# Flamingo gated block on one Trainium2 core: the first normalisation split in natural layout and transposed by a DMA, in a straight program

## The chip, the cores and the metric

The kernel runs on one core of one Trainium2 chip. A core has five engines that work side by side and signal each other with semaphores: PE (TensorE, matmuls and transposes, results to PSUM), DVE (VectorE), ACT (ScalarE), POOL (GpSimd) and SP (SyncE, which here only starts DMAs). The metric is device time in microseconds (us) of one execution, lower is better.

## The reference, cut to what matters

Four sequences of 512 rows of width 512 (2048 rows). Each row's token chooses one of four experts, and the weights of expert e are `ctx_w[e]` (512 x 512), used for all three of its products. Then a small mixture with eight experts of rank 16 follows.

```python
def _layernorm(x, axis=-1, eps=1e-05):
    m = jnp.mean(x, axis=axis, keepdims=True)
    v = jnp.var(x, axis=axis, keepdims=True)
    return (x - m) / jnp.sqrt(v + eps)
# first part, hidden_states = layernorm(x); Wg = Wu = Wd = ctx
for e in range(E):                                   # E = 4
    g = jax.nn.silu(jnp.einsum('bsd,fd->bsf', hidden_states, Wg[e]))
    u = jnp.einsum('bsd,fd->bsf', hidden_states, Wu[e])
    y = jnp.einsum('bsf,df->bsd', g * u, Wd[e])
    out = jnp.where((expert_ids == e)[..., None], y, out)
x = x + jnp.tanh(g_xattn[0]) * out
# second part, on layernorm(x): top 2 of 8 gates w, then
h = jax.nn.relu(jnp.einsum('betd,edr->betr', x, Wd) + bd)     # rank 16
eo = jnp.einsum('betr,erd->betd', h, Wu) + bu
x = x + jnp.tanh(g_ffn[0]) * jnp.einsum('bte,betd->btd', w, eo)
```

## The kernel before, in words

The rows are sorted by expert into 16 tiles of 128 rows (T = 16). A tile that holds rows of two experts is worked on once for each, so there are 19 pairs of tile and expert (NP = T + E - 1). POOL gathers the rows of a tile into `xs` by an indirect DMA and scatters them back at the end.

All products are made of fp16 parts. A factor is split into a high part (rounded to fp16) and a low part (what the rounding left), and a product is three matmuls for each of four blocks of 128: high x high, high x low, low x high (`split_product`, L603 to L605).

For pair k the work is as follows.

- **a(k)**: POOL computes mean and rstd of the tile (`rstd`, L456 to L458) from DVE's `statistics1`. ACT writes the normalised rows `h` (L824). PE transposes them into `ps_hT` (L677), four transposes. ACT copies the high part `hT_hi` from there (L810) and DVE subtracts for the low part `hT_lo` (L1074). PE multiplies (a(k), into `ps_a`).
- ACT takes silu of `ps_a` (L805), DVE multiplies (`prod`, L1068), PE transposes `prod` (L624), ACT and DVE split it (`pT_hi` L783, `pT_lo` L1104).
- **y(k)**: PE multiplies by the expert again (into `ps_y`) and DVE adds the result to the rows (`add_y`, L1086).
- The second part of a tile follows LATE = 3 pairs later: DVE `statistics2` (L1095, L1099), POOL rstd, ACT `h2` (L796, called h in the profile), PE transposes it (`ps_h2T`, L685), split on ACT and DVE (L815, L1110), PE `hidden_product` (L632 to L634), the gates on DVE, ACT (tanh, L801) and POOL (`choice`), PE transposes the weighted hidden values (L697, L698), PE `low_rank_out` (L642 to L645) and DVE adds (L1117).

The order on each engine is written out by hand: `step(i)` has its own list on each engine, and pairs and tiles stand in it with offsets. In step i PE makes, in this order, the hidden product of tile i-6, the transposes of `prod` i-1, a(i), the low-rank output of tile i-7, the transposes of h(i+1), those of h2(i-5), y(i-1) and the small transposes L697 and L698. ACT writes h(i+2) at the end of its step i. DVE makes `hT_lo`(i+1) between `product`(i) and the low part of h2. Each engine runs its list in order, and an instruction that waits holds up all that stand behind it.

The steps up to 6 or so are written one by one, with the preparation of the weights between them: PE transposes the expert weights (L551), ACT takes squares for a scale (L740) and the high parts `w_hi` (L752), DVE the low parts `w_lo` (L952). The later steps go through `pipeline`, which makes hardware loops of two steps for each round; in them the number of the pair is in a register, and column addresses and semaphore values are computed from it. In such loops, DVE writes a cell `gate_cell` (L1049) to carry a second wait ahead of an instruction, and the arrival of tile t of x is passed on by SP through the counter `x_in`.

SP's queue holds, in order: the tokens, the expert weights 0 to 2, a wait for gather 0, the expert weights 3, a wait for gather 1, the two gates, waits for gathers 2 and 3, the eight loads of the small weights of the second part (L397 to L404, semaphore `s_small`), and then the waits for the other gathers. DVE waits for all eight small loads in `router_bias` (L1002), ahead of its step 1, whose first instruction is `pT_lo`(0).

Of the kernel before, what the change touches and what calls it, by code (L numbers as in the profile page):

```python
# [6 lines left out]
def bass_flamingo_gated_kernel(  # L7
# [53 lines left out]
    with ctx:  # L61
# [127 lines left out]
        hT_hi = sb("hT_hi", [P, KC, P], fp16)  # L189
        hT_lo = sb("hT_lo", [P, KC, P], fp16)  # L190
# [122 lines left out]
        def pipeline(eng, step, first, pairs, tiles):  # L313

            def work(i):

                return ([(some(NP, off, i), i + off == 0) for off in pairs]
                        + [(some(T, off, i), i + off == 0) for off in tiles])

            end = max(NP - min(pairs), T - min(tiles))  # L320
            while first < end:
                last = first + 1
                while last < end and work(last) == work(first):
                    last += 1
                if last == first + 1:
                    step(first, first)
                else:
                    odd = (last - first) % 2
                    if odd:
                        step(first, first)  # L330
# [48 lines left out]
        def _(sp):  # L379
# [161 lines left out]
        def _(pe):  # L541
# [70 lines left out]
            def second_product(k, e):  # L612
# [119 lines left out]
        def _(act):  # L732
# [43 lines left out]
            def step(i, i0, meanwhile=None):  # L776
# [29 lines left out]
                if some(NP, 1, i0):  # L806
                    k = i + 1
                    act.wait_ge(hT_done, k + 1)
                    wait_last(act, a_done, k)
                    a(hT_hi[:, :, :], ps_hT[:, :, :], ACT.Copy).then_inc(hT_hi_done, 1)  # L810
# [453 lines left out]
```

## Time and profile before

| | us |
|---|---|
| Median of three runs | 203.82 (203.39 to 203.85) |
| Span of the profiled execution, first to last instruction | 201.4 |
| PE busy in it | 175.0 (87%) |
| DVE busy | 155.7 (77%) |
| ACT busy | 111.9 (56%) |
| POOL busy | 99.7 (50%) |

The time of the profiled execution outside the profiler's span is not recorded by itself; the median of the runs stands 2.4 us above the span, and that is what lies around it.

A group of instructions in the profile has the line, the engine, the operation and the tiles that it writes and reads, then count, busy time, mean duration, and what ended the idle time ahead of it. Matmuls overlap each other, so a PE row of 0.38 us takes less room in the queue: the starts of two neighbours tell how much. PEclk or the granted clock is 1.00 where TensorE runs at its upper level, 2.4 GHz.

### The profile page before, as it was taken

To read this page: it belongs to the slowest core of one execution; us is meant where nothing else is said; L and a number is where in the kernel's file an instruction comes from. 1 tells how busy PE (TensorE), PEld (TensorE's weight loads), DVE (VectorE), ACT (ScalarE), POOL (GpSimd) and SP (SyncE) were. 2 spreads that over 40 slices of the span, in tenths; PEclk is the share of its full clock that TensorE was granted. 3 is DMA by queue.
4 is the path that set the end of the run, shared out by engine and by line. 5 is a ranking of instruction groups with operands and counts; after the bars stand their busy time and mean duration, and the time that the engine had idled before them with its cause. 6 is when DMAs were issued, how large, how long until landed. Compare 5 with 4: busy or idle time off the path is not lost.

```text
span 201.4 us, 4382 instructions
## 1 busy us (share of the span) xinstructions
PE 175.0 (87%) x1074; PEld 104.0 (52%) x1075; DVE 155.7 (77%) x523; ACT 111.9 (56%) x224; POOL 99.7 (50%) x246
## 2 busy tenths in 40 slices
PE   1576896999997989999999999999999999976560
PEld 1564463655553656656656556655665655534310
DVE  4859696697768799889888998797877878678640
ACT  2596599884287166473665726547265561545200
POOL 4478846427246366375553735516244162445641
PEclk9999999999999999999999999999999999999955
DMA  5947572101210201203101011011010100101121
GB/s 135 370 163 231 205 216 69 52 5 20 86 55 0 52 0 52 59 0 104 55 0 54 0 52 52 2 52 52 0 54 0 52 20 33 52 0 55 52 104 52
DMA packets 6784, 13.43 MB, mean 67 GB/s; under 512 B 2392, under 2 KB 2520, under 8 KB 6768
## 3 DMA queue, kind: packets, MB, share of 16 engines
q0 software_dynamic: 2560, 8.39, 12.6%
q1 hardware_dynamic: 4208, 4.86, 7.3%
q8 instruction: 6, 0.10, 0.2%
q14 instruction: 10, 0.08, 0.2%
HBM read 9.06 MB, written 4.19 MB: 66 GB/s over the span
## 4 chain that ended last, share of the span: by engine, by line
PE 44%; issue 18%; POOL 10%; DVE 9%; DMA 7%; ACT 4%; DVEq 3%; SPq 2%; POOLq 1%; ACTq 0%
PE ps_y L603 6%; PE ps_y L605 6%; PE ps_y L604 6%; PE ps_a L603 4%; PE ps_a L605 4%; PE ps_a L604 4%; DMA xs<-in_x_dram,rows_of 4%; ACT h L796 3%; POOL rs L457 3%; PE ps_h2T L685 2%; PE ps_pT L624 2%; DMA bu_nat<-in_L_ffn_bu_dram 2%; POOL hot_slot L432 2%; PE ps_hT L677 2%; POOL xs L439 2%
## 5 line engine op out<-in xcount | busy, mean ns | idle before, releaser
L456 POOL TENSOR_SCALAR ve<-mv 128x1 f32<-128x1 f32 x32 | 7.7, 239 | 62.6 <-DVE mv L1099 51.8
L796 ACT ACTIVATE h<-xs,mrs,rs 128x512 f32<-128x512 f32 (+1 forms) x16 | 21.1, 1317 | 22.4 <-POOL mrs L458 22.4
L783 ACT ACTIVATE pT_hi<-ps_pT 128x512 f16<-128x512 f32 x19 | 11.3, 595 | 36.0 <-PE ps_pT L624 36.0
L603 PE MATMUL ps_y<-w_hi,pT_hi 128*128 x76 | 28.8, 379 | 2.3 <-DVE w_lo L952 1.5
L603 PE MATMUL ps_a<-w_hi,hT_hi 128*128 x76 | 29.1, 382 | 0.7 <-DVE hT_lo L1074 0.6
L604 PE MATMUL ps_a<-w_lo,hT_hi 128*128 x76 | 29.1, 382 | 0.0
L605 PE MATMUL ps_a<-w_hi,hT_lo 128*128 x76 | 29.0, 381 | 0.0
L604 PE MATMUL ps_y<-w_lo,pT_hi 128*128 x76 | 28.8, 379 | 0.0
L605 PE MATMUL ps_y<-w_hi,pT_lo 128*128 x76 | 28.8, 379 | 0.0
L1086 DVE SCALAR_TENSOR_TENSOR xs<-ps_y,y_t,xs 128x512 f32 x19 | 14.3, 750 | 10.2 <-PE ps_y L605 7.7
L529 POOL DMA_INDIRECT out_dram<-xs,rows_of x16 | 17.3, 1083 | 5.9 <-DVE xs L1117 3.5
L457 POOL TENSOR_TENSOR rs<-ve,neg_half 128x1 f32<-128x1 f32 x32 | 18.9, 592 | 2.7
L439 POOL DMA_INDIRECT xs<-in_x_dram,rows_of x16 | 17.0, 1064 | 3.7 <-issue 2.9
L824 ACT ACTIVATE h<-xs,mrs,rs 128x512 f32 (+1 forms) x19 | 15.6, 820 | 4.3 <-POOL mrs L458 3.8
L1068 DVE SCALAR_TENSOR_TENSOR prod<-ps_a,prod_bits,silu 128x512 f32<-128x512 f32 x19 | 14.1, 744 | 1.6 <-ACT silu L805 1.6
L805 ACT ACTIVATE silu<-ps_a,inv_bits 128x512 f32<-128x512 f32 x19 | 12.8, 676 | 4.2 <-PE ps_a L605 4.2
L685 PE MATMUL ps_h2T<-ident,h 128*128 128x128 f32 x64 | 10.2, 281 | 4.2 <-ACT h L796 4.1
L1104 DVE TENSOR_TENSOR pT_lo<-ps_pT,pT_hi 128x512 f16<-128x512 f32 x19 | 13.1, 689 | 0.7 <-ACT pT_hi L783 0.3
L1117 DVE SCALAR_TENSOR_TENSOR xs<-ps_o,out_coef,xs 128x512 f32<-128x512 f32 (+1 forms) x16 | 11.9, 742 | 2.0 <-PE ps_o L645 2.0
L1074 DVE TENSOR_TENSOR hT_lo<-ps_hT,hT_hi 128x512 f16<-128x512 f32 x19 | 12.9, 680 | 0.3 <-ACT hT_hi L810 0.3
L740 ACT ACTIVATE sq_act<-w_nat 128x512 f32<-128x512 f32 x16 | 10.1, 634 | 5.4 <-DMA w_nat<-in_ctx_dram 5.0
L632 PE MATMUL ps_hid<-w_in_hi,h2T_hi 128*128 128x136 f16 x64 | 12.1, 223 | 0.6 <-DVE h2T_lo L1110 0.4
(209 smaller groups left out, 424.0 us busy)
## 6 DMA issues: line engine op xcount, KB each, us to landing
w_nat<-in_ctx_dram SPq DMA_DIRECT2D x4, 1024.0 KB, 7.9
xs<-in_x_dram,rows_of POOLq DMA_INDIRECT x16, 3.6
wd_nat<-in_L_ffn_Wd_dram SPq DMA_DIRECT2D x1, 256.0 KB
wu_nat<-in_L_ffn_Wu_dram SPq DMA_DIRECT2D x1, 256.0 KB
out_dram<-xs,rows_of POOLq DMA_INDIRECT x16, 2.9
b_in<-in_L_ffn_bd_dram SPq DMA_DIRECT2D x1, 64.0 KB
bu_nat<-in_L_ffn_bu_dram SPq DMA_DIRECT2D x3, 16.0 KB
tok_i<-in_itok_BxS_dram SPq DMA_DIRECT2D x1, 8.0 KB, 1.8
```

The costliest lines, as they stand in the source:

```text
L439: g.indirect_dma_start(out=xs[:, t, :], out_offset=None, in_=x_rows[:, :], in_offset=bass.IndirectOffsetOnAxis(ap=rows_of[:, t:t + 1], axi ...
L457: then(g.tensor_tensor(rs[:, n, k:k + 1], ve[:, n, k:k + 1], neg_half[:, :], ALU.pow))
L529: g.indirect_dma_start(out=out_rows[:, :], out_offset=bass.IndirectOffsetOnAxis(ap=rows_of[:, k:k + 1], axis=0), in_=x1[:, k, :], in_offse ...
L603: mm(ps[:, :], lhs_hi[:, kc, :], hi, start=(kc == 0), stop=False)
L604: mm(ps[:, :], lhs_hi[:, kc, :], lo, start=False, stop=False)
L605: last = mm(ps[:, :], lhs_lo[:, kc, :], hi, start=False, stop=(kc == KC - 1))
L685: last = tr(ps_h2T[:, c, :], h2[:, c, :], ident[:, :])
L796: a(h2[:, :, :], x1[:, col(k), :].rearrange("p o (q c) -> p c (o q)", c=KC), ACT.Identity, bias=mrs[:, 1, col(k)], scale=rs[:, 1, col(k)]) ...
L824: a(h[:, :], flat(xs[:, col(tile), :]), ACT.Identity, bias=mrs[:, 0, col(tile)], scale=rs[:, 0, col(tile)]).then_inc(normed1, 1)
L1068: v.scalar_tensor_tensor(prod[:, :], ps_a[:, :], prod_t[:, col(k)], silu[:, :], ALU.mult, ALU.mult).then_inc(prod_done, 1)
L1086: v.scalar_tensor_tensor(flat(x1[:, col(tile), :]), ps_y[:, :], y_t[:, col(k)], flat(xs[:, col(source), :]), ALU.mult, ALU.add).then_inc(x ...
L1104: v.tensor_tensor(pT_lo[:, :, :], ps_pT[:, :, :], pT_hi[:, :, :], ALU.subtract).then_inc(pT_lo_done, 1)
```

## The change: what it does

1. For every pair but the first, h is no longer transposed by PE. ACT writes h (fp32) and then a copy rounded to fp16, `h_parts[k % 2][:, 0]`. DVE subtracts and writes the low part beside it, `h_parts[k % 2][:, 1]` (`h_low`). SP issues one DMA transpose of both parts, 128 rows by 1024 fp16 values (256 KB), into `hT[k % 2]`, which holds high and low parts in the layout that `split_product` reads. Pair 0 goes the old way (`hT_low_0`).
2. The waits follow. PE's a(k) waits for the landing of the transpose (`s_hT[k-1]`) and for `prod_done`; ACT's h(k) for `h_low`(k-1) instead of PE's transposes of k-1; its fp16 copy for its own h(k) and for the transpose of k-2. SP's transpose k waits for `h_low`(k) and for a(k-2).
3. SP's queue gets 18 transposes. The first stands ahead of the eight small loads; the others stand behind them.
4. `h_low`(i+1) stands in DVE's step i ahead of `pT_lo`(i-1); `hT_lo`(i+1) stood behind `product`(i).
5. `pipeline` makes no loops: every step is written out with numbers known when the program is built. The five gate memsets and the counter `x_in` go; `statistics1`(k) waits for its gather itself.

```diff
-        def pipeline(eng, step, first, pairs, tiles):
...
-                    with eng.Fori(0, (last - first) // 2) as n:
-                        step(n * 2 + (first + odd), first)
-                        step(n * 2 + (first + odd + 1), first)
-                first = last
+        def pipeline(step, first, pairs, tiles):
+
+            for i in range(first, max(NP - min(pairs), T - min(tiles))):
+                step(i, i)
...
+            def transpose_h(k):
+
+                sp.wait_ge(h_lo_done, k)
+                wait_last(sp, a_done, k - 1)
+                sp.dma_start_transpose(hT[k % 2][:, :, :, :].rearrange("p s c q -> p (s c) q"),
+                                       h_parts[k % 2][:, :, :].rearrange("p s d -> p (s d)"))\
+                  .then_inc(s_hT[k - 1], 16)
...
-            for t in range(T):
+            for t in range(AHEAD):
                 sp.wait_ge(s_gather[t], 16)
-                sp.sem_inc(x_in, 1)
...
                 if t == AHEAD - 1:
+                    transpose_h(1)
                     sp.dma_start(b_in[:, 0:ER], bd.rearrange("(a e) r -> a (e r)", a=1).to_broadcast([P, ER])).then_inc(s_small, 16)
...
+            for k in range(2, NP):
+                transpose_h(k)
...
-                    pe.wait_ge(hT_lo_done, k + 1)
-                    split_product(ps_a, hT_hi, hT_lo, e_now).then_inc(a_done, 1)
+                    if k == 0:
+                        pe.wait_ge(hT_lo_done, 1)
+                    else:
+                        pe.wait_ge(s_hT[k - 1], 16)
+                    wait_last(pe, prod_done, k)
+                    split_product(ps_a, hT[k % 2][:, 0, :, :], hT[k % 2][:, 1, :, :],
+                                  e_now).then_inc(a_done, 1)
...
-                if some(NP, 1, i0):
-                    k = i + 1
-                    pe.wait_ge(normed1, k + 1)
+                if i == -1:
+                    pe.wait_ge(normed1, 1)
                     for c in range(KC):
                         last = tr(ps_hT[:, c, :], h[:, c * P:(c + 1) * P], ident[:, :])
...
+                    if k:
+                        act.wait_ge(normed1, k + 1)
+                        if k > 2:
+                            act.wait_ge(s_hT[k - 3], 16)
+                        a(h_parts[k % 2][:, 0, :], h[:, :], ACT.Copy).then_inc(h_hi_done, 1)
...
+            def h_low(k):
+
+                dve.wait_ge(h_hi_done, k)
+                v.tensor_tensor(h_parts[k % 2][:, 1, :], h[:, :], h_parts[k % 2][:, 0, :],
+                                ALU.subtract).then_inc(h_lo_done, 1)
...
+                if some(NP, 1, i0):
+                    h_low(i + 1)
                 if some(NP, -1, i0) and not ending:
                     pT_low(i - 1)
...
-                if some(NP, 1, i0):
-                    hT_low(i + 1)
...
             scale(2)
+            h_low(1)
             product(0)
-            hT_low(1)
             statistics1(3)
             router_bias()
```

The queue of SP before, from the gates to the last small load (the names are the tile written and the DRAM input read):

```order
L394 DMA gates_in<-in_g_xattn_dram 128x1 [waits s_gather1]
L395 DMA gates_in<-in_g_ffn_dram 128x1
L397 DMA b_in<-in_L_ffn_bd_dram 128x128 [waits s_gather2,s_gather3]
L398 DMA b_in<-in_L_ffn_br_dram 128x8
L399 DMA wr_nat<-in_L_ffn_Wr_dram 128x32
L400 DMA wd_nat<-in_L_ffn_Wd_dram 128x8x64
```

The small loads come right behind the waits for gathers 2 and 3. And the same place of SP's queue now, to the first of the later transposes:

```order
L385 DMA gates_in<-in_g_ffn_dram 128x1
L371 DMA_TRANSPOSE hT<-h_parts 128x8x128 [waits h_lo_done,s_gather3,s_gather2]
L388 DMA b_in<-in_L_ffn_bd_dram 128x128
L389 DMA b_in<-in_L_ffn_br_dram 128x8
L390 DMA wr_nat<-in_L_ffn_Wr_dram 128x32
L391 DMA wd_nat<-in_L_ffn_Wd_dram 128x8x64
L392 DMA wu_nat<-in_L_ffn_Wu_dram 128x512
L395 DMA bu_nat<-in_L_ffn_bu_dram 8x512 [waits s_const]
L395 DMA bu_nat<-in_L_ffn_bu_dram 8x512 x2
L371 DMA_TRANSPOSE hT<-h_parts 128x8x128 [waits a_done,h_lo_done] x17
```

The first transpose came in, and all eight small loads now stand behind a transpose that waits for DVE.

DVE at the start, ahead of its step 1, as it stands now:

```order
L955 SCALAR_TENSOR_TENSOR w_lo<-ps_wT,scale_w,w_hi 128x512 [waits s_whi]
L945 COPY top_all<-ps_hid 128x1 [waits s_topall]
L946 TENSOR_SCALAR half_exp<-top_all 128x1 [waits s_route]
L948 TENSOR_SCALAR scale_w<-half_exp 128x1 [waits s_route]
L1074 TENSOR_TENSOR h_parts<-h,h_parts 128x512 [waits h_hi_done]
L1062 SCALAR_TENSOR_TENSOR prod<-ps_a,prod_bits,silu 128x512 [waits silu_done]
L1054 BN_STATS st<-xs 128x6 [waits aggr1,s_gather3]
L1057 BN_AGGR mv<-st 128x2 [waits rstd1,stats1]
L1005 TENSOR_SCALAR b_in<-b_in 128x8 [waits s_small]
L1074 TENSOR_TENSOR h_parts<-h,h_parts 128x512 [waits h_hi_done,s_y_t,s_places]
L1102 TENSOR_TENSOR pT_lo<-ps_pT,pT_hi 128x512 [waits pT_hi_done]
```

The first `h_low` stands behind the low parts of expert 1 and the scale of expert 2; the second stands behind the wait for the small loads. Before, `prod` and `hT_lo` stood where `h_low`(1) and `prod` stand now, and nothing stood between `b_in` and `pT_lo`.

## Rows read from the trace of the kernel before

**Rows 1.** Windows of steady steps: us, then busy time and count of each engine, PEclk, DMA
```profile
82.90:91.20 8.30, 8.30 (x55) 5.00 (x54) 7.15 (x26) 4.73 (x9) 4.78 (x13) 1.00 0.12 33
```

**Rows 2.** Timeline of PE in step 7: start us, duration, instruction
```profile
79.47 0.60 PE L677 MATMUL ps_hT<-ident,h 128*128 128x128 f32 x4
79.91 0.60 PE L685 MATMUL ps_h2T<-ident,h 128*128 128x128 f32 x4
```

**Rows 3.** Chain that ended last, whole span: start us, us, what; transposes of h2
```profile
71.57 0.66 PE ps_h2T L685 x4
...
172.65 0.66 PE ps_h2T L685 x4
```

**Rows 4.** Timeline of DVE, steps 6 to 8: start us, duration, instruction, idle before
```profile
75.08 0.75 DVE L1086 SCALAR_TENSOR_TENSOR xs<-ps_y,y_t,xs 128x512 f32 x1 [0.29 <-PE ps_y L605]
...
78.06 0.69 DVE L1104 TENSOR_TENSOR pT_lo<-ps_pT,pT_hi 128x512 f16<-128x512 f32 x1
...
83.37 0.75 DVE L1086 SCALAR_TENSOR_TENSOR xs<-ps_y,y_t,xs 128x512 f32 x1 [0.43 <-PE ps_y L605]
```

**Rows 5.** Timeline of ACT, h2 in a step written out and in a looped one
```profile
78.18 1.32 ACT L796 ACTIVATE h<-xs,mrs,rs 128x512 f32<-128x512 f32 x1 [1.04 <-POOL mrs L458]
...
86.76 1.33 ACT L796 ACTIVATE h<-xs,mrs,rs 128x512 f32 x1 [1.24 <-POOL mrs L458]
```

**Rows 6.** Chain that ended last, 12 to 60 us: the small loads and y(0)
```profile
23.71 0.33 SPq L397
...
24.64 1.12 SPq L399
...
27.65 4.23 DMA bu_nat<-in_L_ffn_bu_dram
...
34.26 0.39 PE ps_y L603
```

**Rows 7.** Timeline of DVE, 24 to 32 us
```profile
24.88 0.75 DVE L952 SCALAR_TENSOR_TENSOR w_lo<-ps_h2T,scale_w,w_hi 128x512 f16<-128x512 f32 x1 [0.85 <-ACT w_hi L752]
...
27.96 0.74 DVE L1068 SCALAR_TENSOR_TENSOR prod<-ps_a,prod_bits,silu 128x512 f32<-128x512 f32 x1
...
31.90 0.17 DVE L1002 TENSOR_SCALAR b_in<-b_in 128x8 f32<-128x8 f32 x1 [1.77 <-DMA bu_nat<-in_L_ffn_bu_dram]
```

**Rows 8.** Timeline of ACT at the start, 23 to 40 us
```profile
23.46 0.81 ACT L824 ACTIVATE h<-xs,mrs,rs 128x512 f32 x1 [2.09 <-POOL mrs L458]
24.18 0.67 ACT L752 ACTIVATE w_hi<-ps_h2T,scale_w 128x512 f16<-128x512 f32 x1
...
34.08 0.86 ACT L824 ACTIVATE h<-xs,mrs,rs 128x512 f32 x1
...
39.83 0.60 ACT L783 ACTIVATE pT_hi<-ps_pT 128x512 f16<-128x512 f32 x1 [0.42 <-PE ps_pT L624]
```

**Rows 9.** Timeline of DVE and of PE in step 3
```profile
47.88 0.69 DVE L1104 TENSOR_TENSOR pT_lo<-ps_pT,pT_hi 128x512 f16<-128x512 f32 x1
...
52.57 0.38 PE L603 MATMUL ps_a<-w_hi,hT_hi 128*128 x1
```

**Rows 10.** DMA issues: engine, count, KB each, us from issue to landing
```profile
w_nat<-in_ctx_dram SPq DMA_DIRECT2D x4, 1024.0 KB, 7.9
xs<-in_x_dram,rows_of POOLq DMA_INDIRECT x16, 3.6
...
tok_i<-in_itok_BxS_dram SPq DMA_DIRECT2D x1, 8.0 KB, 1.8
```

**Rows 11.** Chain that ended last, 56 to 84 us: a(7)
```profile
76.18 0.21 PE ps_a L603
```

**Rows 12.** Window in the tail: us, busy times as in Rows 1, granted clock
```profile
190.00:192.40 2.40, 1.77 (x5) 0.48 (x6) 1.28 (x7) 0.20 (x1) 1.97 (x6) 0.66 0.00 0
```

**Rows 13.** Timeline of PE in the tail: neighbours at the lower clock
```profile
190.79 0.63 PE L643 MATMUL ps_o<-wu_lo,wtT_hi 128*128 128x512 f16 x1
191.21 0.63 PE L644 MATMUL ps_o<-wu_hi,wtT_lo 128*128 128x512 f16 x1
```

More of the change, by code:

```diff
@@ L188, in bass_flamingo_gated_kernel @@
         h = sb("h", [P, D])
-        hT_hi = sb("hT_hi", [P, KC, P], fp16)
-        hT_lo = sb("hT_lo", [P, KC, P], fp16)
+        h_parts = [sb(f"h_parts{b}", [P, 2, D], fp16) for b in range(2)]
+        hT = [sb(f"hT{b}", [P, 2, KC, P], fp16) for b in range(2)]
         silu = sb("silu", [P, D])
@@ L272, in bass_flamingo_gated_kernel @@
         hT_lo_done = sem("hT_lo_done")
+        h_hi_done = sem("h_hi_done")
+        h_lo_done = sem("h_lo_done")
+        s_hT = [sem(f"s_hT{k}") for k in range(1, NP)]
         a_done = sem("a_done")
@@ L311, in some @@
             return 0 <= i + off < n
-        def pipeline(eng, step, first, pairs, tiles):
[L315 to L330, printed above, removed]
-                    with eng.Fori(0, (last - first) // 2) as n:
-                        step(n * 2 + (first + odd), first)
-                        step(n * 2 + (first + odd + 1), first)
-                first = last
+        def pipeline(step, first, pairs, tiles):
+            for i in range(first, max(NP - min(pairs), T - min(tiles))):
+                step(i, i)
         def col(k):
@@ L342, in wait_last @@
         def wait_last(eng, done, k):
-            if not (isinstance(k, int) and k == 0):
+            if k:
                 eng.wait_ge(done, k)
@@ L727, in _ @@
             pe.wait_ge(s_ffn_w, 2)
-            pipeline(pe, step, 7, (-1, 0, 1), (-2 - LATE, -3 - LATE, -4 - LATE))
+            pipeline(step, 7, (-1, 0, 1), (-2 - LATE, -3 - LATE, -4 - LATE))
         @block.scalar
@@ L805, in step @@
                     a(silu[:, :], ps_a[:, :], ACT.Silu, scale=inv_t[:, col(k)]).then_inc(silu_done, 1)
-                if some(NP, 1, i0):
[L807 to L810, printed above, removed]
+                if i == -1:
+                    act.wait_ge(hT_done, 1)
+                    a(hT[0][:, 0, :, :], ps_hT[:, :, :], ACT.Copy).then_inc(hT_hi_done, 1)
                 if some(T, -2 - LATE, i0):
@@ L856, in _ @@
             ffn_high_parts()
-            pipeline(act, step, 5, (-1, 0, 1, 2), (2, -2 - LATE, -3 - LATE, -4 - LATE))
+            pipeline(step, 5, (-1, 0, 1, 2), (2, -2 - LATE, -3 - LATE, -4 - LATE))
         @block.vector
@@ L1045, in ffn_out_low_parts @@
                                        ALU.mult, ALU.subtract).then_inc(s_ffn_w, 1)
-            def gate(n):
-                v.memset(gate_cell[:, n:n + 1], 0.0)
             def statistics1(k):
-                if isinstance(k, int) and k == 0:
-                    dve.wait_ge(s_gather[0], 16)
-                else:
-                    dve.wait_ge(x_in, k + 1)
+                dve.wait_ge(s_gather[k], 16)
                 wait_last(dve, aggr1, k)
-                gate(0)
                 v.bn_stats(st1[:, :], xs[:, col(k), :].rearrange("p o d -> p (o d)")).then_inc(stats1, 1)
@@ L1061, in statistics1 @@
                 wait_last(dve, rstd1, k)
-                gate(1)
                 v.bn_aggr(mv1[:, :], st1[:, :]).then_inc(aggr1, 1)
@@ L1093, in statistics2 @@
                 wait_last(dve, aggr2, k)
-                gate(2)
                 v.bn_stats(st2[:, :], flat(x1[:, col(k), :])).then_inc(stats2, 1)
@@ L1097, in statistics2 @@
                 wait_last(dve, rstd2, k)
-                gate(3)
                 v.bn_aggr(mv2[:, :], st2[:, :]).then_inc(aggr2, 1)
@@ L1140, in step @@
                     dve.wait_ge(hid_done, k + 1)
-                    gate(4)
                     v.max(top8[:, :], hid[:, ER:HC]).then_inc(top_done, 1)
@@ L1209, in _ @@
             top_rows(2)
-            hT_low(0)
+            hT_low_0()
             top_row(2)
@@ L1235, in _ @@
             ffn_out_low_parts()
-            pipeline(dve, step, 6, (-1, 0, 1), (3, -1 - LATE, -2 - LATE, -3 - LATE, -4 - LATE))
+            pipeline(step, 6, (-1, 0, 1), (3, -1 - LATE, -2 - LATE, -3 - LATE, -4 - LATE))
 _INS = ['x', 'itok_BxS_13_99985', 'ctx_2048', 'g_xattn', 'g_ffn', 'L0_ffn_Wr', 'L0_ffn_br',
```

21 lines of the change are left out of this document (11 added, 10 removed).

## The prediction

> **What bounds the kernel now.** I read the windows by step first, then PE's timeline in one step, the chain that ended last, and the DVE and ACT timelines where that chain leaves PE.
>
> In steady steps PE is full: 8.30 us busy of 8.30 at the full clock [rows 1]. Four transposes of h take 0.44 us of that, the distance between the starts of L677 and L685 [rows 2]. But the step is not only PE's. From 71.57 to 172.65 the transposes of h2 start 12 times more [rows 3], so the mean step is 101.08 / 12 = 8.42 us, more than PE's 8.30.
>
> The second limit is a loop. y is done, DVE adds it and takes statistics, POOL makes rstd, ACT writes h2, PE transposes it, and only behind that comes the next y in PE's order. Its length: add_y starts at 75.08 [rows 4], h2 ends at 78.18 + 1.32 = 79.50 [rows 5], 4.42 us; some 0.05 to PE; and from the transposes of h2 at 79.91 [rows 2] to the next add_y at 83.37 [rows 4] 3.46. Together 7.93 us. Step 8 is looped, and there add_y at 83.37 to the end of h2 at 88.09 is 4.72 [rows 4, 5], so the loop is 8.23. The 0.3 us more are register work for addresses, between DVE, POOL and ACT.
>
> At the start the bound is another. DVE waits for the small loads until 31.90, after 1.77 us with nothing to do [rows 7]; the chain goes from SP's first small load at 23.71 through the landing of `bu_nat` to y(0) at 34.26 [rows 6]. From there PE's list is dense, so what delays y(0) delays all of it.
>
> **The change, part by part.**
>
> *Start, added on the path.* The first transpose stands ahead of the small loads and waits for `h_low`(1). When is that?
> - ACT writes h(1) at 23.46, then `w_hi` of expert 1 from 24.18 [rows 8]. The fp16 copy comes between: 0.7 us, by the 0.67 of a `w_hi`. DVE's `w_lo` therefore starts at 24.88 + 0.70 = 25.58 instead of 24.88 [rows 7].
> - DVE needs from 24.88 to 27.96 for four `w_lo` and the scale [rows 7], 3.08 us: now done at 28.66. `h_low`(1) takes 0.68: 29.34. SP sees it at 29.4.
> - X is the time that SP spends on issuing the transpose. No row shows one. Plain issues take 0.33 to 1.12 [rows 6]. The lower end is 0.3, the upper 4.2, the longest time that a small load spends behind its issue [rows 6]. I take 1.5, a little over the longest plain issue, since a transpose has more to cut up.
> - Then the small loads as before: 31.90 - 23.71 = 8.19 us [rows 6, 7]. With fewer gathers beside them this may shrink by up to 1; I take none. DVE's `b_in` comes at 29.4 + 1.5 + 8.2 = 39.1.
> - y(0) follows `b_in` by 34.26 - 31.90 = 2.36, and now `h_low`(2) stands between, 0.6: y(0) at 42.1. The delay is **7.8 us** (5.5 to 10.5 by X and the shrinkage).
>
> The Trainium skill ("DMA: Bandwidth & Descriptors", the section on B0's fast DGE) gives 262,144 sequencer cycles for 8,192 tiles of an on-chip transpose on the older path, 32 each. [...]
>
> What is queued behind the new waits there is covered. ACT's h(2) waits for `h_low`(1), and behind it stand squares, `pT_hi`(0) and the copies of expert 2; these have until 39.1. ACT's h(3) waits for `h_low`(2), which ends at 39.1 + 0.8 = 39.9; it stood at 34.08 [rows 8], so it moves by 5.8. Behind it stand the squares and `pT_hi`(1), which had 0.42 us to spare at 39.83 [rows 8]. With a fp16 copy in place of another they move by about 6, and PE wants `pT_hi`(1) 7.8 later: hidden.
>
> *PE's clock.* PE now stands from about 30.5 to 42 with only a(1) and some transposes, 3 us of work. In the tail, where PE also pauses, the granted clock is 0.66 over 190 to 192.4 [rows 12], a stretch at the lower level, 1.2 GHz, and neighbours stand 0.42 apart [rows 13], twice the distance at the upper level. If the 12 matmuls of y(0) run so, that is 12 x 0.21 = 2.5 us more. The bounds are 0 and 3; I take **1.0**.
>
> *Steady steps, removed from PE.* 8.30 - 0.44 = 7.86 for PE. The loop loses its register work in the straight program, so 7.93 in each step, less two gate memsets of 0.06: 7.87. DVE has 8.29 between add_y and add_y in rows 4 and loses five gates (0.3); `h_low` (0.68) replaces `hT_lo` (0.68) but leaves the full stretch behind the tanh for the slack ahead of it. There `pT_lo` moves from 78.06 to 78.7 and ends at 79.3, before y wants it near 79.95. I take 7.95 a step: 12 x (8.42 - 7.95) = **5.6 us gained**. ACT exchanges one 0.6 us copy for another and has over 3 us idle a step [rows 1].
>
> The Trainium skill ("Runtime: NRT & Kernel Launch", Instruction fetch mechanics) says that straight code streams in unnoticed while a taken branch can force a fetch. The trace agrees as far as steps written out (8.3) and looped ones (8.42 in the mean) go. If it counted the other way, by fetches of the longer program, the gain would shrink.
>
> *Does the transpose arrive in time?* `h_low`(8) would end at 78.7; a(7) starts at 76.18 [rows 11], so a(8) at 76.18 + 7.95 = 84.1: a window of **5.4 us** for waking SP, issue, moving and landing. T is unknown. Its bounds by rows are 1.8 (8 KB landing) and 7.9 (1024 KB landing) [rows 10]; nearest is the gather of 256 KB, 3.6. I take 4.0, as its pieces are smaller. It fits, and nothing is paid.
>
> In steps 2 to 4 the step is only some 6.2 us. Three sets of transposes go, 1.3 us. But `h_low`(4) would end at 47.88 + 0.6 = 48.5 and a(4) starts at 52.57 - 0.44 = 52.1 [rows 9]: a window of 3.6. With T = 4.0 I lose 0.4 again: **0.9 gained**. The two steps behind are bound by the loop in its written-out form: 0.1.
>
> *Sum.* 7.8 + 1.0 - 5.6 - 0.9 - 0.1 = +2.2 us. The profiled span of 201.4 becomes 203.6, and with the 2.4 us around it the time is **206.0**.
>
> **The rivals.**
>
> *Transposes too slow (R1).* If T exceeds 5.4, each steady step waits. From `h_low`(i+1) through a(i+1), y(i+1) and add_y to `h_low`(i+3) are two steps, so a step grows by (T - 5.4) / 2. With T = 7.9 that is 1.25 x 12 = 15 us, some 4 in the early steps and 2.5 more for X: 206.0 + 21.5 = 227. For it: 1024 pieces of 256 bytes are many, nothing like it is in the trace, and one must land within each step. Against it: 256 KB take 3.6.
>
> The Trainium skill speaks for both. "VectorE: DVE Perf Modes", The three transpose paths, gives 1309 ns for one 128 x 128 block by DMA; eight in a row would be 10.5 us, an estimate, and some 245 us in all. "DMA: Bandwidth & Descriptors", Latency and other measured facts, gives 261 GB/s for such transposes, 1 us for 256 KB beside a fixed cost of about 2, and then all fits.
>
> *The start costs less and PE gains all (R2), faster.* The place is SP's queue between 29.4 and `b_in`. With X = 0.4, loads 1 us shorter and no fall of the clock, the delay is 5.7. With T under 3.6 the early steps give 1.3 and the steady ones 12 x (8.42 - 7.88) = 6.5. That is -2.1: 201.7. It decides where the delay, with clock, drops below the gain of 6.6 to 7.9. For it: only X is unseen. Against: 5 us of the delay are DVE and ACT rows.
>
> *Even (R3).* Both sides within 0.6 us: 203.8.
>
> **How the numbers follow.** Forecast (slower by 0.6 to 6 us) 0.46; R1 0.25; R2 0.21; R3 0.08. A change under 0.3%, 0.6 us, can't be told from none here. So faster 0.21, same 0.08, slower 0.71. The likeliest case alone lies in 204.5 to 210. For 8 in 10, the range reaches into R2 to 201.5 and into R1 to 221, which leaves out some 0.05 below and 0.13 above.
>
> **What would show it.** In the new profile: the first transpose issued near 29.4 and `b_in` near 39; y(0) near 42 and its first matmuls 0.4 apart; the h2 transposes every 7.9 to 8.0 us without alternation; no idle PE time ahead of a(k) that the transpose ends. If a(k) waits for the DMA in most steps, R1 holds. If `b_in` comes before 36, R2 does. If the h2 step stays above 8.2, I misread the loop.

## The result, and the profile after

| | time, us (median, range) | ratio to before, 95% |
|---|---|---|
| before | 203.83 (203.39 to 203.88) | |
| after | 209.38 (207.34 to 210.32) | 1.0265 [1.0212, 1.0317] |

The change makes the kernel slower by 5.55 us where the forecast was slower by 2.2. The profiled execution of after is its fastest, 207.34 us with a span of 205.6. Ratios leave out executions over 1.5% above a kernel's fastest, so after, whose executions lie between 206.0 and 210.3 us over two measurements, has 1.0265 in the one and 1.0185 in the other (experiment 12).

The page of after: busy time of the engines, then the two lines of slices with PE's busy tenths and its granted clock, and the packets. The last line is the granted clock of the kernel before.

```profile
PE 172.3 (84%) x1002; PEld 96.2 (47%) x1002; DVE 156.1 (76%) x442; ACT 116.8 (57%) x223; POOL 106.0 (52%) x246
...
PE   1666874699999497999999999999999999986550
...
PEclk9995596799999759999999999999999999999985
...
DMA packets 25797, 18.23 MB, mean 89 GB/s; under 512 B 21400, under 2 KB 21528, under 8 KB 25776
```

```profile
PEclk9999999999999999999999999999999999999955
```

The kernel before has nines up to the tail. After has three dents: slices 4 and 5 (15 to 26 us), 7 and 8 (31 to 41 us), and 14 and 15 (67 to 77 us). The first is no mark of the change: the straight program alone (experiment 1) has it too, and the second profile of after (experiment 12) has not. The second dent is a(1), on PE:

```profile
33.59 0.61 PE L596 MATMUL ps_a<-w_hi,hT 128*128 x1 [3.06 <-DMA hT<-h_parts]
33.99 0.63 PE L597 MATMUL ps_a<-w_lo,hT 128*128 x1
```

It has waited 3.06 us for its transpose, and its matmuls stand 0.43 us apart instead of 0.22. It ends at 38.9 and y(0) starts at 40.69 behind DVE's `w_lo`, so it does not hold up y(0). The third dent is step 5, below.

**The start.** SyncE's queue in the timeline of after, which answers to [rows 6], then DVE in the same stretch [rows 7] and the first matmul of y(0) on PE:

```profile
29.26 1.33 SPq L371 DMA_TRANSPOSE hT<-h_parts  x1
30.64 0.56 SPq L388 DMA_DIRECT2D b_in<-in_L_ffn_bd_dram  x1
...
33.31 1.04 SPq L395 DMA_DIRECT2D bu_nat<-in_L_ffn_bu_dram  x3
```

```profile
28.48 0.68 DVE L1074 TENSOR_TENSOR h_parts<-h,h_parts 128x512 f16<-128x512 f32 x1
...
37.73 0.17 DVE L1005 TENSOR_SCALAR b_in<-b_in 128x8 f32<-128x8 f32 x1 [7.09 <-DMA bu_nat<-in_L_ffn_bu_dram]
```

```profile
40.69 0.39 PE L596 MATMUL ps_y<-w_hi,pT_hi 128*128 x1 [1.80 <-DVE w_lo L955]
```

The transpose is issued at 29.26, and the first small load at 30.64 instead of 23.71. DVE stands 7.09 us where it stood 1.77, and y(0) starts 40.69 - 34.26 = 6.43 us later.

**Step 5.** The transposes of h2(0) on PE in the kernel before:

```profile
63.23 0.66 PE L685 MATMUL ps_h2T<-ident,h 128*128 128x128 f32 x4 [1.42 <-ACT h L796]
```

PE's timeline of after (the last matmul of a(5), the transposes of h2(0), y(4)), then two windows of it with the granted clock as the third number from the end:

```profile
67.25 0.38 PE L598 MATMUL ps_a<-w_hi,hT 128*128 x1
70.43 1.12 PE L682 MATMUL ps_h2T<-ident,h 128*128 128x128 f32 x4 [2.81 <-ACT h L793]
71.34 0.63 PE L596 MATMUL ps_y<-w_hi,pT_hi 128*128 x1
71.77 0.63 PE L597 MATMUL ps_y<-w_lo,pT_hi 128*128 x1
```

```profile
64.70:70.40 5.70, 2.92 (x16) 1.24 (x13) 5.00 (x13) 3.16 (x6) 2.24 (x4) 0.94 0.22 56
70.40:76.70 6.30, 6.27 (x20) 2.90 (x21) 1.44 (x2) 2.60 (x4) 2.12 (x4) 0.51 0.32 78
```

PE stands idle for 2.81 us, where it was 1.42, and comes back at 0.51 of the clock, its lower level of 1.2 GHz: neighbours of y(4) stand 0.43 us apart, in a step that runs at 1.00 in the kernel before.

**The steady steps.** The transposes of h2 in the chain of after [rows 3], a window of one step [rows 1], and the transposing DMAs with their median time to landing [rows 10]:

```profile
97.81 0.57 PE ps_h2T L682 x4
105.79 0.56 PE ps_h2T L682 x4
113.77 0.58 PE ps_h2T L682 x4
```

```profile
105.79:113.77 7.98, 7.98 (x51) 4.50 (x52) 7.47 (x21) 5.03 (x11) 4.90 (x13) 1.00 0.26 68
```

```profile
hT<-h_parts SPq DMA_TRANSPOSE x18, 3.1
```

A step is 7.98 us without alternation. The window has PE busy throughout, but the ends of matmuls are modelled, and what sets the step is the loop of the second part. ACT's h2, its transposes on PE and the next add_y on DVE in after:

```profile
96.35 1.32 ACT L793 ACTIVATE h<-xs,mrs,rs 128x512 f32<-128x512 f32 x1 [1.03 <-POOL mrs L451]
...
97.72 0.42 PEld L682 LDWEIGHTS ps_h2T<-ident,h 128*128 128x128 f32 x4 [0.41 <-ACT h L793]
97.72 0.66 PE L682 MATMUL ps_h2T<-ident,h 128*128 128x128 f32 x4
...
101.23 0.75 DVE L1086 SCALAR_TENSOR_TENSOR xs<-ps_y,y_t,xs 128x512 f32 x1 [0.24 <-PE ps_y L598]
```

h2 ends at 97.67 and its transposes start 0.05 us later, as they do in the two steps behind. From add_y at 93.25 to the end of h2 are 4.42 us, then 0.05, then 3.51 to the next add_y: 7.98.

Starts of y in the two timelines turn all this into a balance (us, after less before):

| stretch | before | after | difference |
|---|---|---|---|
| to y(0) | 34.26 | 40.69 | +6.4 |
| y(0) to y(3) | 21.34 | 21.15 | -0.2 |
| y(3) to y(4) | 8.12 | 9.50 | +1.4 |
| y(4) to y(5) | 8.34 | 10.91 | +2.6 |
| y(5) to y(18) | 105.99 | 100.76 | -5.2 |
| y(18) to the end | 23.35 | 22.59 | -0.8 |

The sum is +4.2, the difference of the spans. The profiled execution of after, its fastest, is only 3.5 us above the median of before, and the medians are 5.55 apart: this trace does not hold the whole of it. The -0.8 at the end goes with the clock of this execution, 0.73 over the last 11.6 us against 0.57 over the last 12.35 in before. In the second profile of after this stretch takes 23.1 us, and in the last kernel of experiment 12 it takes 23.4.

### The profile page after: what moved, and what is told of

Its sections match the earlier page's. It is cut to its first block, busy times and chain, and to the rows that moved or that the text cites. A ratio compares the mean times of both kernels' runs of the same rounds, so it can differ in the third digit from the quotient of the medians.

```text
span 205.6 us, 3989 instructions
## 1 busy us (share of the span) xinstructions
PE 172.3 (84%) x1002; PEld 96.2 (47%) x1002; DVE 156.1 (76%) x442; ACT 116.8 (57%) x223; POOL 106.0 (52%) x246
## 3 DMA queue, kind: packets, MB, share of 16 engines
q0 software_dynamic: 2560, 8.39, 12.5%
## 4 chain that ended last, share of the span: by engine, by line
PE 58%; DVE 12%; POOL 10%; issue 7%; DMA 5%; ACT 2%; SPq 2%; DVEq 1%; POOLq 1%; ACTq 0%
PE ps_y L596 8%; PE ps_y L598 8%; PE ps_y L597 8%; PE ps_a L596 6%; PE ps_a L597 5%; PE ps_a L598 5%; PE ps_h2T L682 4%; PE ps_pT L617 3%; DVE w_lo L955 3%; POOL xs L432 2%; DMA hT<-h_parts 2%; POOL hot_slot L425 2%; DMA bu_nat<-in_L_ffn_bu_dram 2%; POOL rs L450 2%; DVE xs L1086 1%
## 5 line engine op out<-in xcount | busy, mean ns | idle before, releaser
L596 PE MATMUL ps_a<-w_hi,hT 128*128 x76 | 30.5, 402 | 3.8 <-DMA hT<-h_parts 3.2
L793 ACT ACTIVATE h<-xs,mrs,rs 128x512 f32<-128x512 f32 x16 | 21.0, 1314 | 19.6 <-POOL mrs L451 19.6
L596 PE MATMUL ps_y<-w_hi,pT_hi 128*128 x76 | 29.9, 393 | 2.7 <-DVE w_lo L955 1.8
L597 PE MATMUL ps_a<-w_lo,hT 128*128 x76 | 30.4, 400 | 0.0
L598 PE MATMUL ps_a<-w_hi,hT 128*128 x76 | 30.3, 399 | 0.0
L597 PE MATMUL ps_y<-w_lo,pT_hi 128*128 x76 | 29.8, 392 | 0.0
L598 PE MATMUL ps_y<-w_hi,pT_lo 128*128 x76 | 29.8, 392 | 0.0
L682 PE MATMUL ps_h2T<-ident,h 128*128 128x128 f32 x64 | 11.0, 296 | 5.5 <-ACT h L793 5.5
L596 PEld LDWEIGHTS ps_a<-w_hi,hT 128*128 128x128 f16 x76 | 7.7, 102 | 12.3 <-issue 6.1
L596 PEld LDWEIGHTS ps_y<-w_hi,pT_hi 128*128 128x128 f16 x76 | 7.6, 100 | 11.9 <-issue 5.5
L1115 DVE SCALAR_TENSOR_TENSOR xs<-ps_o,out_coef,xs 128x512 f32<-128x512 f32 x16 | 11.8, 738 | 1.5 <-PE ps_o L638 1.5
```

Of the source, the lines that this page charges most:

```text
L596: mm(ps[:, :], lhs_hi[:, kc, :], hi, start=(kc == 0), stop=False)
L597: mm(ps[:, :], lhs_hi[:, kc, :], lo, start=False, stop=False)
L598: last = mm(ps[:, :], lhs_lo[:, kc, :], hi, start=False, stop=(kc == KC - 1))
L682: last = tr(ps_h2T[:, c, :], h2[:, c, :], ident[:, :])
L793: a(h2[:, :, :], x1[:, col(k), :].rearrange("p o (q c) -> p c (o q)", c=KC), ACT.Identity, bias=mrs[:, 1, col(k)], scale=rs[:, 1, col(k)]) ...
```

## The experiments

Each ran five rounds beside the kernel before. Diffs are against after unless another is named.

**1. The straight program alone** (against before: loops written out, gates and `x_in` gone).

```diff
-                    with eng.Fori(0, (last - first) // 2) as n:
-                        step(n * 2 + (first + odd), first)
-                        step(n * 2 + (first + odd + 1), first)
+            for i in range(first, max(NP - min(pairs), T - min(tiles))):
+                step(i, i)
```

> The kernel before with the straight program alone (no loops, no gate memsets, no x_in); h is still transposed by TensorE. Theory A (the two loop-bound steps and the 0.3 us longer second half of each loop pass were the cost of the loop): the steps of 8.29 and 8.6 us become 8.3 throughout, so y(18) comes some 1.5 to 2 us earlier and the ratio to before is 0.990 to 0.994 (201.8 to 202.6 us). Rival (part of the loss of the change comes from the longer code, fetched as it runs): ratio 1.00 or above, with idle time that no semaphore explains.

201.72 us, 0.9883 [0.983, 0.9937]. y(18) at 176.69 against 178.05, the transposes of h2 every 8.29 us from 88.91 to 113.78. So 0.13 of the 8.42 - 7.98 us that the change gains in a step goes with the hardware loops, and 0.31 with the transposes. Theory A holds, though y(18) comes 1.4 us earlier and not 1.5 to 2. One stretch got longer: y(3) to y(4) is 8.48 us against 8.12, because add_y(3) starts 1.01 us behind the start of y(3)'s last matmul, where it was 0.65. The versions with DMA have this too, and no run shows its cause.

**2. The first transpose behind the small loads.**

```diff
                 if t == AHEAD - 1:
-                    transpose_h(1)
...
-            for k in range(2, NP):
+            for k in range(1, NP):
```

> The changed kernel with the first transposing DMA moved behind the small loads in SyncE's order. Theory A (the loss of the early stretch is the position of that DMA ahead of the small loads): y(0) comes at 34.3 to 35.5 us from the span's start, as before, where the change has 40.69; the whole is 5 to 6.5 us shorter than the changed kernel, 203 to 204.5 us, ratio to before 0.996 to 1.003, if the clock still falls in step 5. Rival (the transposes of pairs 2 to 4, whose small packets share the DMA engines with the weight loads, are what holds the loads up): y(0) stays at 38 or later and the ratio at 1.015 or above. A warning: a(1) stands ahead of y(0) on TensorE and now waits for a transpose issued some 5 us later, so y(0) could be held there instead; then 1 to 2 us less are won.

203.53 us, 0.9985 [0.9945, 1.0026]. Moving one line gives back 4.4 to 5.9 us, by the second or the first measurement of after. `b_in` is at 32.01, but y(0) at 37.25 and not at 34.5, for the reason of the warning: a(1) stands 2.63 us for the transpose, PE's row of this kernel:

```profile
33.18 0.39 PE L595 MATMUL ps_a<-w_hi,hT 128*128 x1 [2.63 <-DMA hT<-h_parts]
```

The warning has only half of it. Twelve matmuls at 0.22 us would end near 35.8, but from 34.7 on those of a(1) stand 0.43 apart and y(0) starts right behind them: some 1.5 us of the delay are the clock. With `b_in` at 32.01 and y(0) ahead of 38 the rival is out.

**3. Extra matmuls in the idle time of steps 5 and 6.**

```diff
-            step(5, 5)
+            step(5, 5, meanwhile=dummies(11))
...
-            step(6, 6)
+            step(6, 6, meanwhile=dummies(5))
```

`dummies(n)` issues n matmuls of w_hi by w_hi into the spare bank `ps_hT`; nobody reads them.

> The changed kernel with 11 extra matmuls of 128x128x512 (fp16, results read by nobody) on TensorE behind a(5) and 5 behind a(6), in the idle time of 2.81 and 1.35 us ahead of the transposes of h2. Theory A (the granted clock of 0.51 from 70.4 to 76.7 us follows from that idle time and costs y(4) 12 x 0.21 = 2.6 us and the h2 transposes 0.45): the clock is 1.00 there, y(5) comes 2.5 to 3.2 us earlier, ratio to before 1.010 to 1.014 (206 to 206.7 us). Rival (the clock falls elsewhere by chance in each execution, as the spread of 207.3 to 210.3 us hints): the time stays within 1 us of 209.4. Second rival (the added matmuls delay the transposes of h2): time above 209.4.

207.28 us, 1.0147 [1.009, 1.0203]. PE's timeline of this kernel in step 5, and the window over y(4):

```profile
70.54 2.54 PE L702 MATMUL ps_hT<-w_hi 128*128 128x512 f16 x11
73.52 0.66 PE L682 MATMUL ps_h2T<-ident,h 128*128 128x128 f32 x4 [0.45 <-ACT h L800]
74.02 0.38 PE L596 MATMUL ps_y<-w_hi,pT_hi 128*128 x1
```

```profile
70.50:76.50 6.00, 5.55 (x28) 2.63 (x27) 4.31 (x10) 3.92 (x5) 3.64 (x6) 1.00 0.23 44
```

With eleven matmuls more y(4) to y(5) is 8.35 us and not 10.91, at a clock of 1.00. The ratio alone, with its interval, would not tell this from after's second 1.0185; the traces of all runs do, at the end of experiment 12. y(5) itself came no earlier, at 82.37 against 82.25, since in this execution y(0) to y(1) was 11.08 us, where after's profiled one has 8.40. The time is a little over the 206 to 206.7 expected for that reason: both theory A and the first rival had a part right.

**4. Transposes by DMA from pair 7 only.** Pairs 0 to 6 go by TensorE as before, and all transposing DMAs stand behind the small loads.

```diff
+        K0 = 7
...
-                if i == -1:
-                    pe.wait_ge(normed1, 1)
+                if i + 1 < K0:
+                    pe.wait_ge(normed1, i + 2)
...
-            for k in range(2, NP):
+            for k in range(K0, NP):
```

> Both ways in one straight program: pairs 0 to 6 are transposed by TensorE as before, pairs 7 to 18 by the DMA, whose first transpose stands behind all small loads. Theory A (the gain is 12 steady steps of 0.45 us, the loss is all in the stretch ahead of pair 7): the early stretch is that of the kernel before (y(5) at about 72 us) and the steady steps last 7.98 us, so the ratio is 0.965 to 0.975 (196.7 to 198.7 us). Rival (the early loss is the price of the steady gain, by the clock or by DMA packets): ratio above 0.985.

198.23 us, 0.9734 [0.968, 0.9788]: the fastest of all, 2.7% under before and 4.4 to 5.3% under after. y(0) is at 34.70, y(5) at 72.96 and the steps behind it take 7.98 us. Theory A holds. Of the 0.9 us by which y(5) is later than in before, 0.4 are there at y(0) already and 0.4 lie between y(3) and y(4), as in experiment 1.

**5. The same, TensorE's transposes kept** (against experiment 4).

```diff
+                elif i + 1 < NP:
+                    for c in range(KC):
+                        tr(ps_hT[:, c, :], w_nat[:, 0, c, 0:P], ident[:, :])
```

> The version with pairs 7 to 18 by DMA, but with TensorE still doing four fp32 128x128 transposes in each of these steps (of weights that lie in SBUF, result read by nobody, no wait). Theory A (the steady gain is TensorE's 0.44 us alone, since its order bounds the step): the steps become 8.26 to 8.45 us and the time 201.5 to 203.5 us, ratio 0.990 to 1.000. Rival (the gain comes from ScalarE and VectorE, which no longer read h from PSUM, or from waits that are gone): the steps stay at 8.0 to 8.1 us and the time below 199.8 us.

200.96 us, 0.9909 [0.9872, 0.9945]. Steps of 8.29 to 8.30 us: theory A holds, and what is gained comes out of PE's time. PE's timeline of this kernel shows why it is 0.31 us and not the 0.44 that the transposes take:

```profile
104.21 0.38 PE L638 MATMUL ps_o<-bu,gwT 96*128 96x512 f16 x1
104.43 0.60 PE L678 MATMUL ps_hT<-ident,w_nat 128*128 128x128 f32 x4
104.87 0.60 PE L685 MATMUL ps_h2T<-ident,h 128*128 128x128 f32 x4
```

The extra transposes take 0.44, from 104.43 to 104.87. ACT's h2 ends at 104.47 here and waits 0.4 for PE. Without the extra transposes PE's list would take 8.29 - 0.44 = 7.85 us, and the loop takes 7.98 (the steady steps above): PE then waits for h2, and 0.13 of the 0.44 is lost in that.

**6. Transposes by DMA from pair 2**, the form of experiment 4 with `K0 = 2`.

> Pairs 0 and 1 by TensorE, pairs 2 to 18 by DMA, all transposing DMAs behind the small loads. Theory A (the delay of y(0) is pair 1 alone: its place ahead of the small loads in the changed kernel, its late landing in the version with it behind them): y(0) at 34.3 to 34.9 us, all 6 us of delay gone; the clock still falls in step 5 (idle time of TensorE over 2.5 us ahead of the transposes of h2), so y(5) comes at 74.5 to 75.5 us; 200 to 201.5 us, ratio 0.983 to 0.990. Rival (the DMA packets of pairs 2 to 4 or VectorE's new order delay the weights' parts): y(1) or y(2) over 1 us later than before and a ratio of 0.995 or more.

202.36 us, 0.9894 [0.9851, 0.9937], above the 200 to 201.5 expected. y(0) is at 35.60, 1.3 us later than in before where 0 to 0.6 was expected; most of the delay is gone. In step 5 PE stands 2.81 us again and y(4) to y(5) is 9.54. New is a fall over y(0), ahead of which PE is busy for 0.67 of 3.60 us:

```profile
32.00:35.60 3.60, 0.67 (x4) 0.10 (x2) 2.96 (x6) 3.60 (x8) 1.51 (x2) 1.00 0.46 104
35.60:40.00 4.40, 4.40 (x14) 1.85 (x15) 1.83 (x4) 4.16 (x13) 2.71 (x5) 0.61 0.21 34
```

The rival had y(1) over 1 us late right (45.68 against 43.09) but not the cause, and its ratio of 0.995 isn't reached. Theory A had left this fall out.

**7. The same with the extra matmuls of experiment 3.**

> The same with 11 extra matmuls behind a(5) and 5 behind a(6). Theory A (the clock's fall in step 5 is all that is left against the version with pairs 7 to 18 by DMA): y(5) at 72.5 to 73.2 us and 197.5 to 198.8 us, ratio 0.971 to 0.977. Rival (the clock falls at another place then, as it did at y(0) in the changed kernel with the extra matmuls): 200 us or more.

200.53 us, 0.9847 [0.9804, 0.9891]. Step 5 is cured (8.36 from y(4) to y(5)), the fall over y(0) is not: from y(0) to y(1) 10.09 us. The rival was right on the time.

**8. Ten more extra matmuls ahead of y(0)** (`step(1, 1, meanwhile=dummies(10))`, against experiment 7).

> The version with pairs 2 to 18 by DMA and extra matmuls in steps 5 and 6, with 10 more extra matmuls ahead of y(0), in the idle time of 2.9 us there. Theory A (the fall of the clock over y(0) follows from that idle time, which h's transposes no longer break up): from y(0) to y(1) 8.7 to 8.9 us instead of 10.1, 198.5 to 199.5 us, ratio 0.973 to 0.981. Rival (the fall there is chance or has another cause): y(0) to y(1) stays at 10 us and the ratio at 0.985.

199.08 us, 0.9789 [0.9758, 0.9821]. y(0) to y(1) is 8.38, and theory A holds. With the clock kept up, moving pairs 2 to 6 to DMA as well is no better than leaving them on TensorE (198.23).

**9. h_low in another form** (`scalar_tensor_tensor` with 1.0 for `tensor_tensor`).

> The changed kernel with h_low written as a scalar_tensor_tensor (h times 1.0, less the upper part) in place of a tensor_tensor. Theory P (GpSimd is held up while VectorE reads h and its upper part, both in SBUF, by tensor_tensor): GpSimd's copy arg8f, 708 ns beside h_low against 191 ns in the kernel before, falls below 350 ns, mrs at step 5 takes 0.3 instead of 0.89 us, and h2 ends about 0.5 us earlier there; the ratio to before falls by 0.002 to 0.01 from 1.0265. Rival (it is h_low's duration, not its form, or another user of the memory): the copy stays at 600 ns or more and the time at 207 to 210.5 us.

209.37 us, 1.0226 [1.0165, 1.0286]. GpSimd's copy stays at 538 ns in the mean, exactly as in after. The form doesn't matter, and this theory fell as it was put.

**10. h_low 1.4 us later in the step** (against experiment 4: `h_low(i + 1)` behind `statistics1(i + 3)`).

> The version with pairs 7 to 18 by DMA, with h_low moved behind statistics1 in VectorE's order, some 1.5 us later in each step. Theory P (GpSimd's copy arg8f takes 0.71 us and not 0.19 because h_low runs beside it, in whichever form): the copy falls to 190 to 250 ns, and whatever stands beside h_low on GpSimd then is slower instead. In time, theory A (the transpose lands some 2 us before TensorE wants it) expects the steps of 7.98 us kept, 197.5 to 198.9 us. Rival (there is less slack than that, since the landing takes up to 4.1 us): TensorE waits for the DMA in most steps, steps of 8.2 us or more, above 200 us.

200.10 us, 0.982 [0.9787, 0.9852]. Groups of GpSimd in after, then in this kernel (mean ns behind the busy time):

```profile
L484 POOL CAST arg8f<-arg 128x8 f32<-128x8 uint32 x16 | 8.6, 538 | 3.8 <-DVE arg L1143 3.8
...
L489 POOL TENSOR_SCALAR half_second<-slot_no,arg8f 128x8 f32<-128x8 f32 x16 | 5.0, 314 | 0.0
```

```profile
L489 POOL TENSOR_SCALAR half_second<-slot_no,arg8f 128x8 f32<-128x8 f32 x16 | 7.1, 445 | 0.0
...
L484 POOL CAST arg8f<-arg 128x8 f32<-128x8 uint32 x16 | 3.0, 188 | 3.7 <-DVE arg L1145 3.7
```

The copy is fast again, and what now stands beside h_low is slow. On time the rival was nearer: PE waited for a transpose three times, 1.7 us in all, and the steps are 8.0 to 8.8. A transpose is issued at 114.97 here and wanted some 4.0 us later (a(k) starts at 119.39 after a wait of 0.42); landings reach 4.6.

**11. Each transpose twice** (against experiment 4, the second into a spare tile, both waited for).

> The version with pairs 7 to 18 by DMA, with each transpose issued twice (the second into a spare tile) and waited for twice. Theory A (a transpose costs SyncE 1.2 us, lands 3.1 us after its issue and has some 2 us of slack): the second lands 1.2 to 1.5 us after the first, still in time, steps of 7.98 us and 197.5 to 199 us. Rival (transposes are slow enough that two in a row pass the limit, or their packets hold up the gathers and scatters): TensorE waits for the DMA, above 200 us.

203.91 us, 0.9916 [0.9883, 0.9949], theory A refuted: the waits of PE in this kernel (us in all, times, longest) are

```profile
PE ps_a L602 <- DMA hT<-h_parts: 4.9, 6, 1.4
```

The slack is smaller than I thought. In experiment 4 a transpose is issued at 111.6 and a(k) wants it at 116.8, 5.2 us; landings take 3.0 to 3.2 there. With two in a row they take up to 5.3, and the second starts 1.3 later.

**12. After once more, and after with both idle stretches filled** (experiment 3 and the 10 matmuls of experiment 8).

> The changed kernel as it is, once more, for a second profile. Its first profiled execution was 207.3 us, its median 209.4. Theory A (most executions have a second fall of the clock, over y(0), which the first profiled one had not): median 209 to 210 us, executions in groups some 2 us apart, and a profile of 209 us or more would show y(0) to y(1) at about 11 us, against 8.4 in one of 207. Rival (the 2 us lie elsewhere, in transposes that land late or in the small loads): a profile of 209 us with 8.4 us from y(0) to y(1).

207.95 us, 1.0185 [1.0126, 1.0245], single executions from 206.03 to 210.22: a lower median than the 209 to 210 expected. The profiled one, 209.64 us, is like the median of the first measurement. Its PE timeline at y(0) and a window:

```profile
41.27 0.60 PE L596 MATMUL ps_y<-w_hi,pT_hi 128*128 x1 [3.68 <-DVE w_lo L955]
42.52 0.63 PE L596 MATMUL ps_y<-w_hi,pT_hi 128*128 x1
```

```profile
41.00:46.30 5.30, 5.03 (x12) 1.94 (x13) 2.10 (x5) 4.04 (x14) 2.14 (x4) 0.50 0.22 39
```

y(0) runs at 0.50 of the clock, y(0) to y(1) takes 10.93 us against 8.40. That is 2.5 us that the first profiled execution did not have, as theory A said, and y(4) to y(5) is 9.76, so the second fall is still there, shorter. The traces also differ ahead of y(0). Here a(1) came back to the upper level half way, ended at 37.6, and PE stood 3.68 us. In the first profile a(1) stayed at the lower level to its end and PE stood 1.80.

> The changed kernel with 10 extra matmuls ahead of y(0), 11 behind a(5) and 5 behind a(6). Theory A (the clock costs the median execution 2 us at y(0) and 2.6 at y(4)): 204.3 to 205.5 us, ratio to before 1.004 to 1.010, and executions closer together. What is left against before is the start delay of 6.4 less the steady gain of 5.2 and some 0.8 in the tail, plus 0.6 to 1 in step 5. Rival (only the fall at y(4) is real for the median): 206.5 to 207.5 us, as with the matmuls in steps 5 and 6 alone.

205.21 us, 1.009 [1.006, 1.012], executions from 204.13 to 205.75, as theory A said. The interval lies below both of after's. With both falls gone the spread shrinks from 4 us to 1.6, and what is left is 1.8 us over before: y(0) 6.5 late (40.81), y(3) to y(4) 1.0 longer, 5.2 gained behind y(5) and 0.2 between y(0) and y(3); the tail is that of before.

All profiled executions together show what the idle time does in step 5:

| y(4) to y(5), us | kernels |
|---|---|
| 8.33 to 8.34 | before and the five with TensorE's transposes in these steps (experiments 1, 4, 5, 10, 11) |
| 9.54 to 10.91 | the five with DMA and no extra matmuls there (after twice, experiments 2, 6, 9) |
| 8.34 to 8.36 | the four with DMA and extra matmuls there (experiments 3, 7, 8 and the last) |

At y(0) it is less regular. With the ten extra matmuls y(0) to y(1) is 8.38 and 8.39. Without them, where h(2) goes by DMA, it is 10.08 to 11.08 in five profiles, but 8.40 in the first profile of after and 8.59 in experiment 2, and in both of these a(1) ends at the lower level just ahead of it.

## Why the prediction was wrong in size

The second profile of after is the nearer to the medians, so I set the sum against it. To the forecast of +2.2 us the start adds -0.8, PE's clock +3.2, the early steps +0.7, y(3) to y(4) +1.0, the steady steps +0.5 and the tail -0.3. That is +6.5, the difference of the spans (207.9 and 201.4).

- **The start** was right in mechanism and a little too large: 6.4 to 7.0 us against 7.8. Each point held: ACT's copy delayed `w_lo` (25.39 against 24.88), h_low(1) ended at 29.16, X is 1.33 against 1.5. The loads took less, from 29.26 + 1.33 = 30.59 to `b_in` 7.14 us, not 8.19.
- **PE's clock is the step that failed.** The prediction put one fall, over y(0), with 0 to 3 us, and took 1.0. The runs show two places. One is y(0), up to 2.5 us, absent in some executions. The other is y(4), for which there was no term: 1.4 to 2.6 us from y(4) to y(5), and 0.25 to 0.4 ahead of it in h2's transposes. Together that is 3.0 us in the first profile of after and 4.2 in the second. Filling both idle stretches takes the kernel to 205.21 us, from 209.38 by the first measurement and 207.95 by the second: 2.7 to 4.2 us for the term that was 1.0.

  I asked only where PE's pause grows because its data come later. It grows as well where work is taken out of it: step 5 has a pause for the loop add_y, statistics, h2 in the kernel before, and h's four transposes stood ahead of it. Of the growth from 1.42 to 2.81 us some 0.35 came with the straight program (1.77 in experiment 1, at a clock that stayed up), 0.44 are the missing transposes, and 0.6 are the longer loop of the last point below. No run tells the last two apart.
- **The steady gain** was right, in mechanism too: 5.2 measured for 5.6. The prediction had PE's list at 7.86 and the loop at 7.87, and took 7.95. PE's list is 7.85 by experiment 5, and the loop, now the bound, is 7.98. Its 0.3 us more in a looped step are gone as well: add_y to the end of h2 takes 4.42 us in after, as in the step written out before.
- **The early steps** gained 0.2 us from y(0) to y(3), where I had 0.9. The first gained 0.4; y(1) to y(3) is 12.75 against 12.51. In before PE was the bound there, as I thought: it is busy for all 6.23 us from y(2) to y(3). In after it is busy for 6.13 of 6.37, because with its work gone others took over. The chain of after ahead of a(4):

```profile
54.03 0.70 DVE h_parts L1074
...
54.75 4.10 DMA hT<-h_parts
```

The transpose landed 4.10 us behind `h_low`(4), close to the T of 4.0. In the step ahead PE stood 0.39 us for DVE's `prod`; the prediction's account of these steps has no wait for DVE.
- **The transposes** land in 3.1 us for the 4.0 taken, and the largest of after is 4.1. R1 did not happen. It was nearer than this looks, as experiments 10 and 11 show. R2's cheap start needs another place in the queue; with that, and with TensorE's transposes where they keep it busy, it goes further than R2 put it (experiment 4).
- **Not in the sum: y(3) to y(4).** Of the +1.4 us there 0.4 are the longer stretch of experiment 1, 0.4 the clock, and 0.6 a longer loop: from add_y to the end of h2 it takes 5.14 us (65.23 to 70.37), against 4.56 in before and in experiment 1. These are GpSimd's `mrs` there and DVE's h_low beside it, in after:

```profile
68.16 0.89 POOL L451 TENSOR_SCALAR mrs<-mv,rs 128x1 f32<-128x1 f32 x1
```

```profile
68.23 0.68 DVE L1074 TENSOR_TENSOR h_parts<-h,h_parts 128x512 f16<-128x512 f32 x1
```

In the kernel before that `mrs` takes 0.29 us. y(3) to y(4) is 9.1 us at the full clock with DMA in this step (experiments 7, 8 and the last) and 8.48 with TensorE's transposes (experiment 4). So 0.6 us belong to the DMA way there; that they are this `mrs` follows from the rows and from what experiment 10 shows of other instructions, and no run took h_low away in step 5 alone.
- **Outside the span** the prediction added 2.4 us. In after it is 207.34 - 205.6 = 1.7, which hid some of the error.

## What to carry to other kernels

When work leaves an engine that also waits, ask of each wait what stood in it or ahead of it. TensorE's transposes cost 0.31 us a step where it was full. In step 5, where it was not, taking them out was part of what lengthened its pause from 1.42 to 2.81 us, and y(4) behind it ran at half the clock. When one bound is shortened, ask also how far away the next one is: here the loop stood 0.13 us above the PE list that was left. Move such work only in the stretch where the engine is the bound, and put the new DMA behind all that the start needs in its queue. Where executions of one kernel scatter by some 2 us, take a second profile before the balance is made.

## What the hardware showed beyond that

- A DMA transpose of 256 KB in fp16, SBUF to SBUF, keeps SyncE's queue for 1.23 us (1.33 at times) and lands 3.0 to 4.1 us after its issue in after, up to 5.3 where two are issued in a row (experiment 11).
- VectorE's h_low reads two operands in SBUF, and a short GpSimd instruction that starts within 0.07 us of it lasts until it ends, or up to 0.14 us longer: the copy's 0.19 us becomes 0.71 (96.26 to 96.97, `h_low` to 96.92). The mean of 538 ns is the same in either form of `h_low`. `pT_lo`, with one operand in PSUM, does not do that: in before the copy at 103.19 stands inside `pT_lo` (103.16 to 103.85) and takes 0.19. The Trainium skill ("SBUF — State Buffer", SBUF: two separate sides) says that an operation of VectorE with two SBUF inputs and a GpSimd one that reads SBUF exclude each other for a whole instruction; the trace agrees as far as `h_low` keeps its 0.68 us and the GpSimd instruction lasts longer. By that rule the prediction could have asked for it.
- Four fp32 transposes of 128 x 128 take 0.44 us of PE's queue where it does not wait, behind fp16 matmuls as well as behind other transposes (experiment 5).
- The granted clock differs between executions of one kernel: of two profiles of after, one has y(0) at 0.50 and the other at 1.00.
